# Feed-forward weights of a fused attention and butterfly feed-forward kernel: transposed and split in the attention's last superblock, and kept in the rows of q and k

## What is computed

```python
xn = layernorm(x)
qkv = (xn @ W_qkv + b_qkv).reshape(B, D, 3, H, p).transpose(2, 0, 3, 1, 4)
attn = einsum('bhij,bhjp->bhip', softmax(einsum('bhip,bhjp->bhij', q, k)), v)

h = einsum('bsd,dh->bsh', xn, W_exp) + b_exp        # 256 -> 1024
h = butterfly(h, up_weights)                        # 10 stages of 2x2 mixes
h = gelu(h + up_bias)
h = butterfly(h, down_weights)
y = einsum('bsh,hd->bsd', h, W_con) + b_con         # 1024 -> 256
return x + attn + y + down_bias
```

## Time and profile before

| what | value |
|---|---|
| median of 3 runs | 5677.05 us (5672.97 to 5677.72) |
| the profiled execution, its own time | 5674.86 us |
| its span | 5673.1 us |
| mean granted clock of TensorE | 0.992 of full speed |
| busy: TensorE, ScalarE, VectorE, POOL | 99%, 88%, 86%, 9% |
| the attention's last sums end | about 5289.5 us |
| first feed-forward matmul | 5307.9 us |

### The profile page before, as it was taken

How to read it: one execution, slowest core, us unless ns; L and a number is a source line. 1 busy time by engine, 2 the same in 40 slices (tenths; PEclk the granted TensorE clock), 3 DMA queues, 4 the chain that set the end, 5 groups by cost and what they waited for, 6 DMA issues and landing times. The chain is left out here.

```text
span 5673.1 us, 97332 instructions
## 1 busy us (share of the span) xinstructions
PE 5605.1 (99%) x35880; PEld 2613.5 (46%) x35880; DVE 4884.6 (86%) x9104; ACT 4977.2 (88%) x9651; POOL 524.8 (9%) x482
## 2 busy tenths in 40 slices
PE   8799999999999999999999999999999999999999
PEld 5444444444444444444444444444444444444698
DVE  6689999999999999999999999999999999996233
ACT  3489999999999999999999999999999999999544
POOL 2245564000000000000000000000000000000000
PEclk9889999999999999999999999999999999999999
DMA  8611111000000000000000000000000000000111
GB/s 288 200 43 43 50 54 42 21 21 19 14 16 21 21 21 21 15 21 21 21 18 14 16 21 21 21 20 16 21 21 21 17 12 20 21 21 2 34 44 41
DMA packets 232761, 197.02 MB, mean 35 GB/s; under 512 B 171752, under 2 KB 192616, under 8 KB 220520
## 3 DMA queue, kind: packets, MB, share of 16 engines
q1 hardware_dynamic: 228848, 168.00, 10.4%
q0 software_dynamic: 3456, 23.07, 1.4%
HBM read 128.07 MB, written 60.82 MB: 33 GB/s over the span
## 5 line engine op out<-in xcount | busy, mean ns | idle before, releaser
L646 ACT ACTIVATE probs<-psum 128x512 f32<-128x512 f32 x8192 | 4222.6, 608 | 294.8 <-PE psum L843 292.8
L708 DVE TENSOR_REDUCE maxima<-psum 128x1 f32<-128x512 f32 x6036 | 3966.7, 686 | 364.7 <-PE psum L821 255.6
L821 PE MATMUL psum<-k_rows,q_rows 48*128 48x512 f32 x7042 | 2494.3, 455 | 0.6 <-ACT spill L670 0.6
L857 PE MATMUL psum<-probs,v_cols 128*32 128x512 f32 x16384 | 2184.7, 605 | 0.5
L843 PE MATMUL psum<-q_rows,k_rows 50*128 50x512 f32 x8192 | 2061.2, 424 | 0.0
L821 PEld LDWEIGHTS psum<-k_rows,q_rows 48*128 48x128 f32 x7042 | 1176.6, 184 | 1248.8 <-DVE maxima L704 809.6
L843 PEld LDWEIGHTS psum<-q_rows,k_rows 50*128 50x128 f32 x8192 | 1266.5, 186 | 135.0 <-ACT probs L646 44.5
L704 DVE CUSTOM_DVE_ANT_0 merged<-psum,spill 128x512 bf16<-128x512 f32 x1006 | 684.8, 681 | 2.7 <-issue 1.9
L670 ACT ACTIVATE spill<-psum 128x512 f32<-128x512 f32 x1006 | 601.0, 597 | 23.9 <-PE psum L821 23.6
L857 PEld LDWEIGHTS psum<-probs,v_cols 128*32 128x32 f32 x16384 | 323.3, 108 | 622.0 <-issue 325.8
L821 PEld LDWEIGHTS psum<-k_diff,q_rows 48*128 48x128 f32 x1006 | 184.6, 183 | 843.0 <-DVE maxima L708 787.7
(11 more groups left out here) (94 smaller groups left out, 2067.0 us busy)
## 6 DMA issues: line engine op xcount, KB each, us to landing
q_rows<-q_parts SPq DMA_DIRECT2D x128, 256.0 KB
q_parts<-parts SPq DMA_DIRECT2D x32, 512.0 KB, 6.0
k_parts<-parts SPq DMA_DIRECT2D x32, 512.0 KB, 3.7
k_rows<-k_parts SPq DMA_DIRECT2D x64, 256.0 KB
q_rows<-q_parts SPq DMA_DIRECT2D x128, 128.0 KB
planes<-in_up_planes POOLq DMA_DIRECT2D x10, 1024.0 KB, 11.3
planes<-in_down_planes POOLq DMA_DIRECT2D x10, 1024.0 KB, 5.4
y<-in_x SPq DMA_DIRECT2D x16, 512.0 KB, 6.0
```

The source lines that it names most:

```text
L646: nc.scalar.activation(probs[:, 2 * (u % 2) + half, BANK * g:BANK * g + BANK], ps_s[:, r % 4, :], ACT.Exp).then_inc(s_exp, 1)
L708: nc.vector.tensor_reduce(largest, region(use), axis=AX_X, op=ALU.max).then_inc(s_region_free, 1)
L821: nc.tensor.matmul(region(use_of[n, j]), q_rows[m % 4][lower:lower + ROWS, P * t:P * t + P], keys[lower:lower + ROWS, :], start=True, stop ...
L857: last = nc.tensor.matmul(ps_o[VW * g:VW * g + VW, :], v_cols[:, KT * (head % 2) + UNITS * half + at, :], probs[:, 2 * (u % 2) + half, BAN ...
```

## The change

The second block's programs now do the preparation of the weights, in its last superblock (`LAST` = unit 1008):

- TensorE: at the end of each of units 1008 to 1015 two transposes of `w_down_t` (`turn_weights`), into banks 4 to 6 in turn; at the end of unit 1017 the bias row (`turn_bias`), into bank 4.
- VectorE: in its step for each of these units the split of a part of `w_up` (2 parts) and of `w_down` (8 parts), and in the tenth the bias addition. The high parts of `w_up`, which ScalarE made, are VectorE's too. The first of them waits until the scores of superblock 62 are done.
- SP: the load of the up bias stands behind the last placing of maxima in the second block.
- The split weights lie in `q_rows` 0 to 2 and `k_rows` 0. These tiles are now made at the start and kept to the end; `planes` and `fold` are made after the first block's scratch is given up. So tiles get other addresses.

The semaphores of the preparation are made in the second block (left out below). The third block begins with its loads of x, and TensorE waits only for weights (done) and for the split of x.

```diff
...
         w_down_t = sb("w_down_t", [P, KD, HID])
-        planes = sb("planes", [P, 2, 4, PAIRS], until=before_ffn)
-        fold = sb("fold", [P, 3, PAIRS], until=before_ffn)
-        q_rows = [sb("q_rows0", [P, QB], F32R, until=before_ffn)]
-        k_rows = [sb("k_rows0", [P, HALF_N], F32R, until=before_ffn)]
+        q_rows = [sb(f"q_rows{n}", [P, QB], F32R) for n in range(3)]
+        k_rows = [sb("k_rows0", [P, HALF_N], F32R)]
+        bias_up = sb("bias_up", [P, 2, HT])
         k_diff = [sb("k_diff0", [P, BANK], F32R, until=before_ffn)]
...
         probs = sb("probs", [P, 4, QG * BANK], until=before_ffn)
+        planes = sb("planes", [P, 2, 4, PAIRS], until=before_ffn)
+        fold = sb("fold", [P, 3, PAIRS], until=before_ffn)
         v_cols = sb("v_cols", [P, 2 * KT, VW], until=before_ffn)
-        q_rows += [sb(f"q_rows{n}", [P, QB], F32R, until=before_ffn) for n in range(1, 4)]
+        q_rows += [sb("q_rows3", [P, QB], F32R, until=before_ffn)]
         k_rows += [sb("k_rows1", [P, HALF_N], F32R, until=before_ffn)]
...
         FIN = 3
...
+        w_up_high, w_up_low = (q_rows[n][:, :].rearrange("p (k n) -> p k n", k=KD) for n in (0, 1))
+        w_down_high, w_down_low = (rows[:, :].rearrange("p (m d) -> p m d", m=HT) for rows in (q_rows[2], k_rows[0]))
+        LAST = UNITS_ALL - UNITS
+        def turned_weights(m):
+            return psum[:, 4 + m % 3, 0:D]
...
+                sp.dma_start(bias_up[:, 0, :], up_bias_columns).then_inc(s_bup, 16)
                 sp.wait_ge(s_neg_in, 2 * 16 * SUPER)
...
                     nc.vector.reciprocal(recip[:, :], o_t[:, :, HD]).then_inc(s_recip, 1)
+                def split_w_up(k):
+                    if k == 0:
+                        dve.wait_ge(s_evac, SUPER - 2)
+                        dve.wait_ge(s_score, 2 * QG * LAST)
+                    nc.vector.tensor_copy(w_up_high[:, k, :], w_up[:, k, :]).then_inc(s_wu_high, 1)
+                    dve.wait_ge(s_wu_high, k + 1)
+                    nc.vector.tensor_tensor(w_up_low[:, k, :], w_up[:, k, :], w_up_high[:, k, :].bitcast(F32),
+                                            ALU.subtract).then_inc(s_wu, 1)
+                def split_w_down(m):
+                    dve.wait_ge(s_wt_ps, m + 1)
+                    nc.vector.tensor_copy(w_down_high[:, m, :], turned_weights(m)).then_inc(s_wt_high, 1)
+                    dve.wait_ge(s_wt_high, m + 1)
+                    nc.vector.tensor_tensor(w_down_low[:, m, :], turned_weights(m), w_down_high[:, m, :].bitcast(F32),
+                                            ALU.subtract).then_inc(s_wt, 1)
+                def add_bias():
+                    dve.wait_ge(s_bup, 16)
+                    dve.wait_ge(s_bias_ps, 1)
+                    nc.vector.tensor_tensor(bias_up[:, 1, :], bias_up[:, 0, :], psum[:, 4, 0:HT], ALU.add).then_inc(s_bias, 1)
...
                             invert(s - 1)
+                    if s == SUPER - 1 and u < KD:
+                        split_w_up(u)
+                    if s == SUPER - 1 and u < HT:
+                        split_w_down(u)
+                    if s == SUPER - 1 and u == HT + 1:
+                        add_bias()
                     if s >= 0 and u == QT - 1:
...
                         pairs(n, i)
+                def turn_weights(m):
+                    if m == 0:
+                        pe.wait_ge(s_evac, SUPER - 2)
+                        pe.wait_ge(s_region_free, vector_uses[use_of["neg", SUPER - 1]])
+                    if m >= 3:
+                        pe.wait_ge(s_wt, m - 2)
+                    for k in range(KD):
+                        last = nc.tensor.transpose(turned_weights(m)[:, P * k:P * k + P], w_down_t[:, k, P * m:P * m + P], ident[:, :])
+                    last.then_inc(s_wt_ps, 1)
+                def turn_bias():
+                    pe.wait_ge(s_wt, HT)
+                    for n in range(HT):
+                        last = nc.tensor.matmul(psum[:, 4, n:n + 1], w_up[0:1, 2, P * n:P * n + P], one[0:1, 0:1],
+                                                start=True, stop=True)
+                    last.then_inc(s_bias_ps, 1)
                 piece(PAIRED - 1, DIFFERENCE)
...
                     sums(u, 1)
+                    if LAST <= u < LAST + HT:
+                        turn_weights(u - LAST)
+                    if u == LAST + HT + 1:
+                        turn_bias()
...
         hidden_low = sb("hidden_low", [P, HT, BANK], F32R)
-        w_up_high = sb("w_up_high", [P, KD, HID], F32R)
-        w_up_low = sb("w_up_low", [P, KD, HID], F32R)
-        w_down_high = sb("w_down_high", [P, HT, D], F32R)
-        w_down_low = sb("w_down_low", [P, HT, D], F32R)
-        bias_up = sb("bias_up", [P, 2, HT])
         ps_h = psum[:, 0:4, :]
...
         s_xp_high = sem("xn_high_parts")
         s_xp = sem("xn_split")
         s_xnt2 = [sem(f"xn_transposed_loaded{n}") for n in range(2)]
...
             def _(sp):
-                sp.dma_start(bias_up[:, 0, :], up_bias_columns).then_inc(s_bup, 16)
                 def load(c, p):
...
-                for m in range(HT):
-                    if m == 4:
-                        for n in range(HT):
-                            last = nc.tensor.matmul(ps_d[:, 0, n:n + 1], w_up[0:1, 2, P * n:P * n + P], one[0:1, 0:1],
-                                                    start=True, stop=True)
-                        last.then_inc(s_bias_ps, 1)
-                    if m >= 4:
-                        pe.wait_ge(s_wt, m - 3)
-                    for k in range(KD):
-                        last = nc.tensor.transpose(ps_h[:, m % 4, P * k:P * k + P],
-                                                   w_down_t[:, k, P * m:P * m + P], ident[:, :])
-                    last.then_inc(s_wt_ps, 1)
                 pe.wait_ge(s_wt, HT)
                 pe.wait_ge(s_wu, KD)
-                pe.wait_ge(s_bias, 1)
...
             def _(act):
-                for k in range(KD):
-                    nc.scalar.copy(w_up_high[:, k, :], w_up[:, k, :]).then_inc(s_wu_high, 1)
                 nc.scalar.activation(warm[0:1, 1:2], one[0:1, 0:1], ACT.Gelu)
...
-                def w_down_high_part(m):
-                    dve.wait_ge(s_wt_ps, m + 1)
-                    nc.vector.tensor_copy(w_down_high[:, m, :], ps_h[:, m % 4, 0:D]).then_inc(s_wt_high, 1)
-                w_down_high_part(0)
-                for m in range(HT):
-                    if m % 4 < 3:
-                        w_down_high_part(m + 1)
-                    dve.wait_ge(s_wt_high, m + 1)
-                    nc.vector.tensor_tensor(w_down_low[:, m, :], ps_h[:, m % 4, 0:D], w_down_high[:, m, :].bitcast(F32),
-                                            ALU.subtract).then_inc(s_wt, 1)
-                    if m == 3:
-                        w_down_high_part(4)
-                for k in range(KD):
-                    dve.wait_ge(s_wu_high, k + 1)
-                    nc.vector.tensor_tensor(w_up_low[:, k, :], w_up[:, k, :], w_up_high[:, k, :].bitcast(F32),
-                                            ALU.subtract).then_inc(s_wu, 1)
                 split_xn(0, 0, 0)
-                dve.wait_ge(s_bup, 16)
-                dve.wait_ge(s_bias_ps, 1)
-                nc.vector.tensor_tensor(bias_up[:, 1, :], bias_up[:, 0, :], ps_d[:, 0, 0:HT], ALU.add).then_inc(s_bias, 1)
```

More of the change, by code:

```diff
@@ L507, in attention_and_butterfly_ffn @@
         FIN = 3
+        s_bup = sem("up_bias_loaded")
+        s_wt_ps = sem("w_down_transposed")
+        s_wt_high = sem("w_down_high_parts")
+        s_wt = sem("w_down_split")
+        s_wu_high = sem("w_up_high_parts")
+        s_wu = sem("w_up_split")
+        s_bias_ps = sem("bias_row_turned")
+        s_bias = sem("bias_added")
+        w_up_high, w_up_low = (q_rows[n][:, :].rearrange("p (k n) -> p k n", k=KD) for n in (0, 1))
[3 more added lines that the diff above has]
+            return psum[:, 4 + m % 3, 0:D]
         def wait_for_stores(engine):
@@ L916, in attention_and_butterfly_ffn @@
         hidden_low = sb("hidden_low", [P, HT, BANK], F32R)
-        w_up_high = sb("w_up_high", [P, KD, HID], F32R)
-        w_up_low = sb("w_up_low", [P, KD, HID], F32R)
-        w_down_high = sb("w_down_high", [P, HT, D], F32R)
-        w_down_low = sb("w_down_low", [P, HT, D], F32R)
-        bias_up = sb("bias_up", [P, 2, HT])
         ps_h = psum[:, 0:4, :]
         ps_d = psum[:, 4:8, :]
[L926 to L931, removed]
         s_xp_high = sem("xn_high_parts")
         s_xp = sem("xn_split")
-        s_bias_ps = sem("bias_row_turned")
-        s_bias = sem("bias_added")
         s_xnt2 = [sem(f"xn_transposed_loaded{n}") for n in range(2)]
```

## The result

The changed kernel takes 5664.5 us (median of 22 runs, 5661.5 to 5672.3) and the kernel before beside it 5675.9 (22 runs, 5672.8 to 5678.0): 11.4 us less. The ratio worked out over all runs is 0.9984 (95% interval 0.9978 to 0.9990); it isn't the quotient of the medians (0.9980), and by it the gain is 9.1 us, between 5.7 and 12.5. The forecast was 5673 with a range from 5668.

What follows compares the result with a forecast made beforehand. The prediction took the 13.42 us weight preparation before the first feed-forward matmul as the chain's attackable part, with attention's TensorE-ScalarE loop without slack. -7.1 + 1.4 + 1.6 = -4.1 us from 5677.05 gave 5673, range 5668 to 5680.

Steps and rivals of the forecast that it cites:

- The chain and what is late next: Feed-forward block's start: preparation leaves the chain, the load of x and its split are late next; gain 7.1 us.
- The loop has no slack: Attention's last superblock: TensorE and ScalarE wait on each other in a loop, so the bias row is charged in full.
- The pair of transposes, 0.18 us a unit: End of eight units in the last superblock: two f32 transposes, partly hidden behind the sums, cost 1.4 us in all.
- The bias row, 1.6 us: Tenth unit of the last superblock: TensorE's bias row, 3.50 us at the slow clock, costs 1.6; ends 1.6 and 3.5.
- The clock: First feed-forward chunk: its slow start at 1.2 GHz, 1.8 us, stays; bounds 0.5 less, 1.8 more.
- Sum of the move: Whole change: -7.1 + 1.4 + 1.6 = -4.1 us; at best -5.9, at worst +2.8.
- the third rival: Placement decides: new addresses and code make attention instructions slower or faster, 16 us either way, 5657 or 5689; chance 0.06.
- "faster": Whole kernel: a measured gain beyond the 11.4 us (0.2%) that can be told from no change; chance 0.03.

Runs made afterwards that it cites:

- after_no_gap: The changed kernel with bias_up's 64 bytes allocated ahead of everything, against the kernel before: 5672.7 / 5673.9 us, ratio 0.9998.
- pad_weights: The kernel before with one unused tile of 64 bytes per partition ahead of the four split weights, nothing else: 5674.4 / 5673.9 us, ratio 1.0002.
- x_gap: Change's placement without its move, bias_up behind hidden_low, 64 bytes ahead of xnt2, 4032 ahead of gelus, against the kernel before: 5679.0 / 5673.0 us, ratio 1.0009.

## Why the prediction was wrong

- **The chain and what is late next**: right. Forecast 6.3 us from the block's start to the first matmul, measured 6.15; gain 7.3, forecast 7.1 (6.4 to 7.2).
- **The loop has no slack**: right. The insertions add to the last superblock in full, 4.87 us by its length.
- **The pair of transposes, 0.18 us a unit**: mis-sized. It took 0.36, 2.9 us for eight instead of 1.4, within the ends given (0.03 to 0.49). The step that failed here is the one that let 0.12 us hide behind the sums as with the small bf16 transpose: the f32 pair starts as late as the score did (1.00 us behind the sums' start). And the pair alone was priced at 2 x 0.109 = 0.22 us, the distance from start to start in a row of eight; two cost 0.36 to the next score. The Trainium skill's page "TensorE: Matmul & The Clock Gate", Part 4 (PE-mode transpose), gives some 275 ns for a transpose in one kernel's context, which as an estimate would have made 4.4 us of the sixteen; the trace shows 2.9, so the truth lay between the page and my row.
- **The bias row, 1.6 us**: somewhat too small. It took 1.87 us of TensorE's time and 1.9 of the loop's in the changed kernel. In after_no_gap it held TensorE for the same 1.87 us, but the last superblock took 69.52 us, 0.95 more than in the changed kernel, and all of it from the row on; why isn't shown.
- **The clock**: taken as no change, and the end given for it, 1.8 us more, held. The first pass took 12.72 and 12.76 us before, and 12.60, 13.96 and 13.99 in the three profiles of the changed kernel, in the mean 0.8 more. That this belongs to the move isn't shown: it took 13.86 in pad_weights, which has the whole preparation at home, and 12.48 in after_no_gap, which has it all moved.
- **Sum of the move**: -7.3 + 4.9 is -2.4 us, with the 0.8 of the first pass -1.6; the forecast was -4.1. after_no_gap, which has the move without the new distance, is 1.2 us under before by the medians. By its profile it is -7.0 (first matmul 6.42 us behind the block's start) + 5.8 (last superblock) - 0.2 (first pass) = -1.4.
- **The placement**: this is what made the prediction wrong. It was the third rival, at 0.06, and priced for an instruction of the attention. The step that failed is that the feed-forward passes behind the first matmul were held to stay as they are: 22.42 us a chunk became 22.32 or 21.89. In the prediction's sum they have no term. The change takes 1.6 or 8.5 us off through this, and by their times 16 of its first 22 executions are of the second kind (one of that kind was profiled, and two of the other). Why a distance of 64 bytes changes the pace is open. The transposing and splitting has no part in this: the 64 bytes of bias_up between two groups of tiles do it, and with them moved elsewhere it is gone.
- **Range and chances**: the effect, 11.4 us, is at the edge of what I called no change, and I gave "faster" 0.03. 1.1 us of the distance from 5673 to 5664.5 is the base: I started from 5677.05, the median of three runs, where 22 give 5675.9. From that base the range would begin at 5667, still above what was measured.

## What to carry to other kernels

When a change moves or reorders tiles, price the work that reads them, not only the instructions that move: measure the change's placement alone, and the move with the old distances. And look at what an idle head of a stage can hide before moving work out of it: here 5.4 us of TensorE's work fitted under a load at home, while in the attention's tight loop nothing of it was hidden (4.87 us for what TensorE did in 8 x 0.36 + 1.87 = 4.75).

## What the runs showed of the hardware

- The pace of the fp32r passes of this kernel, in which TensorE is busy throughout, changed with the distance between the addresses of stationary and moving operand within a partition, at distances below 256 bytes (modulo 4096). 96 matmuls of 128 x 256 took 11.51 us at distances of 0, 256, 512 and 1024 bytes (and multiples of 4096 more), 11.27 to 11.52 at 96, at 128 and with the sign turned, and 10.91 or 11.31 at 64: 0.120 to 0.114 us each. The up pass has its own values, 10.90 to 11.21 us for 48 matmuls of 128 x 512, and they don't follow from its own two operands alone (x_gap).
- At 64 bytes the changed kernel has two paces, each held from the first down pass to the end of the execution in its three profiles (10.91 or 11.31 us a down pass), at the same granted clock of 1.00.
- The f32 transposes behind sums on 32 columns started as late as the score did there before (1.00 us behind the sums' start), while the small bf16 one started 0.12 us sooner than a score (0.42 instead of 0.54).
